# Score products on halves of the array's columns, every mask written ahead, and a new order of steps in an attention loop

## What is computed

```
h = x W^T + b + LoRA(x)
q, k, v = h @ ((qw - 8) * scales)      # per group of 128 rows; 32, 8, 8 heads of 128
q, k = rope(q), rope(k)                # by the token's place
scores = q k^T / sqrt(128), masked where key > query
ctx = softmax(scores) v
x = x + ctx @ ((qw_o - 8) * scales_o)
x = x + FFN(LoRA2(x))                  # layer norm, two layers with 8-bit rounding, GELU
```

## Time and profile before

| | |
|---|---|
| median of 3 runs | 568.68 us (568.56 to 568.96) |
| the profiled execution | 569.7 us, span 567.9 us |
| TensorE busy, clock granted | 542.2 us (95%), 1.00 |
| VectorE, ScalarE, GpSimd busy | 485.0, 363.0, 400.2 us |
| DMA | 51.93 MB, mean 91 GB/s |

### The profile page before, as it was taken

How to read it: one execution, slowest core, us unless ns; L and a number is a source line. 1 busy time by engine, 2 the same in 40 slices (tenths; PEclk the granted TensorE clock), 3 DMA queues, 4 the chain that set the end, 5 groups by cost and what they waited for, 6 DMA issues and landing times.

```text
span 567.9 us, 10485 instructions
## 1 busy us (share of the span) xinstructions
PE 542.2 (95%) x3135; PEld 425.0 (75%) x3139; DVE 485.0 (85%) x626; ACT 363.0 (64%) x940; POOL 400.2 (70%) x410
## 2 busy tenths in 40 slices
PE   6999989999999999999999999999999999987885
PEld 3555768888888888888888888888888888865432
DVE  3553859997999799979997999799979998976897
ACT  3573567657665766576657665766576656665895
POOL 3005577799779977997799779977997799851063
PEclk9999999999999999999999999999999999999999
DMA  8752435422442244124512451245124312200003
GB/s 289 180 123 76 123 88 160 113 56 58 137 124 51 62 133 126 43 65 133 128 37 66 134 132 33 61 136 136 34 61 135 97 34 61 80 1 1 1 20 129
DMA packets 38172, 51.93 MB, mean 91 GB/s; under 512 B 12100, under 2 KB 20452, under 8 KB 38148
## 3 DMA queue, kind: packets, MB, share of 16 engines
q1 hardware_dynamic: 35652, 46.94, 31.3%
q10 hardware_dynamic: 2016, 3.48, 1.9%
q0 software_dynamic: 480, 1.22, 0.7%
HBM read 28.55 MB, written 2.10 MB: 54 GB/s over the span
## 4 chain that ended last, share of the span: by engine, by line
PE 80%; DVE 10%; issue 3%; DMA 2%; ACT 2%; POOL 2%; ACTq 0%; SPq 0%; DVEq 0%; POOLq 0%
PE pair L1378 23%; PE pair L1379 23%; PE flow L1367 9%; PE flow L1494 9%; PE flow L1486 4%; PE pair L1315 4%; DVE y_max L1191 2%; DVE raw_v L1081 1%; PE flow L1372 1%; DMA stage<-in_x 1%; PE flow L1315 1%; DMA swap_q<-raw_q 1%; DVE rope_c L1203 1%; DVE ctx_lo L1102 1%; DVE probs L1203 1%
## 5 line engine op out<-in xcount | busy, mean ns | idle before, releaser
L1095 DVE SCALAR_TENSOR_TENSOR accT<-pair,so_now,accT 128x1024 f32<-128x1024 f32 x125 | 157.2, 1274 | 14.8 <-PE pair L1379 13.9
L1081 DVE SCALAR_TENSOR_TENSOR raw_q<-pair,sc_now,raw_q 128x1024 f32<-128x1024 f32 x90 | 115.4, 1283 | 6.2 <-ACT raw_q L777 2.8
L560 POOL TENSOR_TENSOR probs<-probs,rowinv 128x512 f32<-128x512 f32 x64 | 66.8, 1044 | 65.4 <-DVE rowinv L1068 65.4
L722 ACT ACTIVATE probs<-flow,negmax 128x128 f32<-128x128 f32 x248 | 87.6, 369 | 32.8 <-DVE negmax L1049 32.8
L1378 PE MATMUL pair<-ctx_hi,wo 128*128 128x512 f32 x256 | 104.9, 410 | 2.8 <-issue 1.5
L1378 PE MATMUL pair<-h_hi,wq 128*128 128x512 f32 x240 | 100.0, 417 | 0.3 <-ACT raw_q L777 0.3
L1379 PE MATMUL pair<-ctx_lo,wo 128*128 128x512 f32 x256 | 100.2, 392 | 0.0
L1379 PE MATMUL pair<-h_lo,wq 128*128 128x512 f32 x240 | 94.1, 392 | 0.0
L529 POOL TENSOR_TENSOR rope_s<-swap_q,consts 128x512 f32<-128x512 f32 x62 | 80.2, 1293 | 9.2 <-DMA swap_q<-raw_q 9.2
L541 POOL TENSOR_TENSOR qT<-rope_c,rope_s 128x512 f32<-128x512 f32 x62 | 79.3, 1280 | 4.4
L529 POOL TENSOR_TENSOR rope_c<-raw_q,consts 128x512 f32<-128x512 f32 x62 | 78.8, 1293 | 0.0
(11 more groups left out here) (242 smaller groups left out, 966.3 us busy)
## 6 DMA issues: line engine op xcount, KB each, us to landing
swap_q<-raw_q SPq DMA_DIRECT2D x62, 256.0 KB, 3.7
wq_i<-in_L_attn_qw_q SPq DMA_DIRECT2D x8, 1024.0 KB, 5.6
wo_i<-in_L_attn_qw_o SPq DMA_DIRECT2D x32, 256.0 KB, 2.6
swap_k<-raw_k SPq DMA_DIRECT2D x14, 256.0 KB, 3.6
wkv_i<-in_L_attn_qw_k SPq DMA_DIRECT2D x8, 256.0 KB, 3.7
wkv_i<-in_L_attn_qw_v SPq DMA_DIRECT2D x8, 256.0 KB, 4.0
stage<-in_x ACTq DMA_DIRECT2D x4, 256.0 KB, 5.7
probs<-in_L_ffn_w ACTq DMA_DIRECT2D x4, 256.0 KB, 8.2
```

What stands on the lines that cost most here:

```text
L560: pool.tensor_tensor(pr, pr, rowinv[:, f, :].unsqueeze(2).broadcast_to([P, HB, P]), ALU.mult).then_inc(probs_done, 1)
L722: e = act.activation(probs[:, 0, f, seq(b)], bank[:, seq(b)], ACT.Exp, bias=negmax[:, f, b:b + 1], accum_out=rowsum[:, f, b:b + 1])
L1081: dve.scalar_tensor_tensor(out=into, in0=flat(pair[pair_of(h, (kind, j), last)][:, :, :]), scalar=sc_now[:, scale_slot(kind, h), j:j + 1], ...
L1095: dve.scalar_tensor_tensor(out=a, in0=flat(pair[pair_of(h, (O, c), last)][:, :, :]), scalar=so_now[:, (h if c == 0 else h - 1) % 2, c:c + ...
```

## The change

- **Scores on column halves.** Per pair of sequences b, b+1 four products: the later 64 queries of each over all 128 keys, then the earlier 64 over the first 64 keys. The tokens of even sequences stand turned (64 to 127 first), so that the two later halves fall on different column halves of the array and of the bank. The masked quarter isn't computed.
- **Turned tokens.** x of the even sequences is loaded, and their output stored, in two halves; the tables of cosine, sine and mask get a second, turned copy (1035 instead of 651 columns).
- **Mask.** ScalarE seeds it for all heads in the loop (SEEDED = 4): in head 3 after the copy of the values. The mask product stays for the first and the last scores.
- **Order.** PERIOD, and the lists of all five engines, are written out anew, head by head.

```
+            else:
+                for here, there in zip(HALVES, halves_of(b)):
+                    eng.dma_start(x_nat[b][here, :], x[b, there, :]).then_inc(d_x[b], 16)
...
-        SEEDED = REP - 1
+        SEEDED = REP
...
-        PERIOD = [[(Q, 0), (O, 1), (Q, 1), (Q, 2), (Q, 3), (K, 0), (O, 2), (O, 3), (K, 1), (O, 0)],
-                  [(Q, 0), (O, 1), (Q, 1), (Q, 2), (Q, 3), (K, 2), (O, 2), (O, 3), (K, 3), (O, 0)],
-                  [(Q, 0), (O, 1), (Q, 1), (Q, 2), (Q, 3), (V, 0), (V, 1), (O, 2), (O, 3), (V, 2), (O, 0)],
-                  [(Q, 0), (O, 1), (Q, 1), (Q, 2), (Q, 3), (V, 3), (O, 2), (O, 3), (O, 0)]]
+        PERIOD = [[(Q, 0), (O, 1), (Q, 1), (Q, 2), (K, 0), (Q, 3), (O, 2), (K, 1), (O, 3), (O, 0)],
+                  [(Q, 0), (O, 1), (Q, 1), (Q, 2), (K, 2), (O, 2), (Q, 3), (O, 3), (K, 3), (O, 0)],
+                  [(Q, 0), (O, 1), (V, 0), (Q, 1), (Q, 2), (V, 1), (O, 2), (Q, 3), (O, 3), (V, 2), (O, 0)],
+                  [(Q, 0), (O, 1), (Q, 1), (V, 3), (Q, 2), (Q, 3), (O, 2), (O, 3), (O, 0)]]
...
+                def tile(b, late):
+
+                    rows, keys = halves_of(b)[late], slice(0, P) if late else halves_of(b)[0]
+                    t = HB * f + b
+                    return pe.matmul(bank[rows, seq(b)][:, keys], qT[:, par, seq(t)][:, rows], kT[:, seq(t)][:, keys],
+                                     start=False, stop=True, skip_group_check=True)
+
+                for b in range(0, HB, 2):
+                    tile(b, 1)
+                    tile(b + 1, 1)
+                    tile(b + 1, 0)
+                    mm = tile(b, 0)
...
+                        if h == 3:
+                            act.wait_ge(v_kept, 2 * (g + 1) + f + 1)
+                        else:
+                            act.wait_ge(ctx_split, 2 * n + f + 1)
+                        act.activation(per_pair(flow[f][:, :]), on_each_pair(tri), ACT.Copy).then_inc(mask_seeded, 1)
```

More of the change, by code:

```diff
@@ L816, in body @@
[L816 to L826 removed]
+                        round_kv()
@@ L1498, in values_ahead @@
                     def values_ahead(f):
-                        if h == 3 and not last:
-                            if f == 0:
-                                pe.wait_ge(dve_drained, drains_by(g, h, (V, 3), first, last))
-                            pe.wait_ge(ctx_split, 2 * n + f + 1)
-                            turn_values(f, flow[f])
+                        if last:
+                            return
+                        if f == 0:
+                            pe.wait_ge(dve_drained, drains_by(g, h, (V, 3), first, last))
+                        pe.wait_ge(ctx_split, 2 * n + f + 1)
+                        for b in range(HB):
+                            mm = pe.matmul(flow[f][:, seq(b)], raw_v[:, f, seq(b)], ident, is_transpose=True,
+                                           start=(b == 0), stop=(b == HB - 1), skip_group_check=True)
+                        mm.then_inc(vT_done, 1)
                     def scores_ahead(f):
@@ L1533, in body @@
                         context(0)
-                    else:
+                        context(1)
+                        scores_ahead(0)
+                        scores_ahead(1)
+                        output(0)
+                    elif last and h == 3:
+                        output(1)
+                        output(2)
+                        output(3)
+                        turn_probs(0)
+                        turn_probs(1)
+                        context(0)
+                        context(1)
+                        output(0)
+                    elif h == 0:
+                        project(Q, 0)
+                        output(1)
+                        project(Q, 1)
+                        project(Q, 2)
+                        project(K, 0)
+                        turn_probs(0)
+                        turn_probs(1)
+                        project(Q, 3)
+                        context(0)
+                        context(1)
+                        output(2)
+                        project(K, 1)
+                        output(3)
+                        scores_ahead(0)
+                        scores_ahead(1)
+                        output(0)
+                    elif h == 1:
+                        project(Q, 0)
+                        output(1)
+                        project(Q, 1)
+                        project(Q, 2)
+                        project(K, 2)
+                        turn_probs(0)
+                        output(2)
@@ L1542, in body @@
                         project(V, 0)
+                        project(Q, 1)
+                        project(Q, 2)
+                        turn_probs(0)
                         project(V, 1)
-                    if h == 3:
-                        project(V, 3)
-                    context(1)
-                    if not (last and h >= 2):
+                        output(2)
+                        project(Q, 3)
+                        turn_probs(1)
+                        context(0)
+                        context(1)
@@ L1562, in body @@
-                    output(0)
-                    if not (last and h == 2):
+                        scores_ahead(0)
+                        values_ahead(1)
+                        output(0)
                         scores_ahead(1)
```

497 lines of the change are left out of this document (349 added, 148 removed).

## The result

The change made the kernel slower: **575.31 us** (574.86 to 575.80, 4 runs) against 568.76 us (568.56 to 568.96, 4 runs), a ratio of 1.0115 [1.0098, 1.0133]. The forecast of 564.2 us had the wrong sign, and the time lies above its range. The profiled execution took 575.8 us with a span of 573.7, so the two traces differ by 5.8 us of span.

What follows compares the result with a forecast made beforehand. TensorE's own stream was taken as the bound, busy 95% of the span. From 568.7 us: loop -5.5, early scores +0.3, last head's pair +0.1, input loads +0.6, giving 564.2; range 558.5 to 572.

Steps and rivals of the forecast that it cites:

- The input loads: At the start: two issues of about 0.45 us instead of one for sequences 0 and 2; 0 to 1.5 late, taken 0.6.
- sign of being wrong: The prediction called itself wrong if the period moved over 1.5 us either way, or the start shifted by more than 1.5.
- The last group: First and last groups counted as 1.2 groups' worth beside six whole ones, each 0.77 us less: -5.5 us in all.
- The tiles: Score products on column halves: a half takes 0.68 us against 0.89, 1.7 us less in a group.
- the visits: Entering and leaving the column form: 0.148 us in, 0.20 out, 5 visits, 1.7 us a group, eating the tiles' gain.
- rival 4: Score halves, issue pace: 16 records at 57 ns make 0.91 us, tiles bring nothing, kernel 577; chance 0.05.
- The mask: In the loop: two products fewer, -0.45 us on TensorE a group; head 3's half 1 seed 0.4 us late.
- The value turn: Head 3's value turns: the 0.5 us wait for V's last drain goes, since that drain now lies earlier.
- The stalls: TensorE's waits in a group of the new order: 1.2 us, from turns, contexts, V's last step and the mask seed.
- rival 3: Loop: small waits take back TensorE's gain, period stays at 57.0 us, kernel 569.2; chance 0.15.
- 56.0 to 56.7: Sign expected in the profile after: a loop period of 56.0 to 56.7 us.
- Rival 2: Loop: VectorE falls 1 us further behind, TensorE waits for buffer pairs; period 57.4 us, kernel 572; chance 0.20.

Runs made afterwards that it cites:

- the best version: Changed kernel, x loaded whole and turned by TensorE's transposes, last group's buffer pairs given by steps present, head 3's mask product back; q step not moved: 568.59 us, ratio 0.9984.
- all_mended_product: Changed kernel, x loaded whole and turned by TensorE, last group's pairs by steps present and q step earlier, head 3's mask product back: 568.60 us against 569.52, ratio 0.9977.
- after_whole_scores: Changed kernel with each score product on the whole array again, order, tokens and tables kept: 574.87 us, ratio 1.0086 to the kernel before.
- before_tiles: Kernel before, in its own order and masks, with column halves, turned tokens and split loads: 580.43 us, ratio 1.0201.
- after_last_rotated: Changed kernel, in the last group q's last step ahead of the turns and buffer pairs given out by the steps present: 573.20 us, ratio 1.0058 to the kernel before.
- turned_identity: Changed kernel with x loaded whole and even sequences turned by TensorE's transposes with an exchanged identity: 570.11 us, ratio 1.0006 to the kernel before.

## Why the prediction was wrong

**The input loads: the step that failed most.** The forecast took 0.6 us, "0 to 1.5 late", for two more issues of 0.45 on ScalarE's queue. The runs showed 4.3. Two things were left out. One is that both transfers of a sequence have to land: the first turns of x started at 6.91 us where they had at 4.90, and those of sequence 1 at 9.87 where they had at 6.57. The other is that GpSimd waits for sequence 1 before it issues any of the other four loads. I read the chain up to the fourth x and stopped there; TensorE didn't wait for the fourth after the change. GpSimd's path ended, before, with an issue at about 8.6 and 7.2 us to landing, at 15.8, only 1.2 ahead of the turn that uses it; after, at 21.16. The step had a mechanism that covered one queue, where the change touched two. It also had TensorE turning at the old pace; in the trace its turns took twice as long, and by itself that path was 3.96 late. What makes the two transfers land so late isn't settled: sequence 1 was issued at 2.50 instead of 1.67 and landed 3.3 us later, so that the issues explain 0.8; the rest lies in the transfers. The prediction's own sign of being wrong, a start that shifts by more than 1.5, came.

**The last group: a step that wasn't there.** The forecast counted "1.2 worth in the first and last" as whole gains. The last group has no K and V steps, and the new order leans on them: they stand between exponentials and turns. It lost 2.7 us, of which the pairs make 0.8 (the wait of 0.86 us) and the mask 0.4; 1.5 are left in the best version, and their cause stays open. The waits for the normalisation (1.07 and 0.42) look like the missing K steps, but giving TensorE the q step there, with the pairs mended, removed these waits and not the loss: other waits took their place (all_mended_product, 37.43 against 37.22 without the moved step). So filling those gaps isn't enough; what bounds this group wasn't isolated.

**The tiles: right.** "A half done in 0.68, 0.148 in and 0.20 out" came as 0.67, 0.146 and 0.203. The forecast that the visits eat the tiles' gain is shown by after_whole_scores (net 0.09 us a group) and before_tiles. The Trainium skill (TensorEngine Tiling (Array Packing), Theoretical Speedup) promises up to 2x; the half went from 0.89 to 0.67, 1.3x, which is no more than the left-out quarter of the work gives, before the drains that its Key Properties name took it back. The trace agrees with the drain: a visit costs 0.35 us, in which the prediction counted the first weight loads too.

**The issue pace: rival 4 fell.** 16 records in 0.67 us are 42 ns each, below the 57 ns of the earlier trace rows. The Trainium skill (TensorE: Matmul & The Clock Gate, section "Wait — 56ns, not 53.3ns?") has about 62 ns per matmul with hardware decoding off; 42 ns is below that, so that figure doesn't bound this kernel.

**The mask: right in kind, wrong in size.** The forecast had "-0.45 on TensorE" against "0.4 us late", a gain of 0.05. The wait was 0.63 beyond the way in, and the product put back gave 0.22 us a group. The term that was mis-sized is the chain behind the value turn. The step that failed is "0.20 + 0.60 + 0.60 + 0.10": copy and seed took their 0.60 each, but from the seed's end (246.95 + 0.60 = 247.55) to the scores at 247.77 it was 0.22 and not 0.10, and the whole chain (0.20 + 0.63 + 0.60 + 0.22) 1.65 where I had 1.50.

**The value turn: right.** Its wait of 0.5 has gone.

**The stalls: too few.** With 36.4 of steps, 5.4 of score halves (8 x 0.67), 1.7 of visits (5 x 0.35), 7.1 of contexts, 3.55 of turns and 0.89 of value turns, a group's stream is 55.1, so 56.79 has 1.7 us of stalls where I had 1.2. Of the 0.5, 0.2 are the mask's, and 0.25 stand in front of one turn of half 0 that waits for GpSimd's normalisation (280.85, 0.48 behind a product that streams for 0.23), which the walk didn't have. The period came out 0.29 shorter instead of 0.77, which over 7.2 groups is 3.4 us of the miss; 56.79 lies between the forecast's 56.35 and the 57.0 of rival 3, outside the 56.0 to 56.7 that was to show the forecast.

**The tail: not foreseen.** The stretch in which the granted clock fell, in the windows view of after:

```profile
530.00:534.50 4.50, 4.49 (x26) 1.79 (x19) 3.38 (x11) 3.54 (x10) 0.00 (x0) 1.00 0.00 0
534.50:538.00 3.50, 3.28 (x13) 2.04 (x13) 3.10 (x10) 2.58 (x5) 0.00 (x0) 0.51 0.00 0
```

For 3.4 us the clock is at its lower level, 1.2 GHz (0.51 of 2.4), after a stretch in which TensorE was busy without a break. The same seven products and the turns behind them, first before, then after:

```profile
530.45 1.67 PE L1644 MATMUL pair<-ffT,ident_b 128*128 128x512 bf16 x7
...
533.81 0.66 PE L1605 MATMUL pair<-consts,accT 128*128 128x128 f32 x4 [0.50 <-DVE stage L1181]
```

```profile
536.26 2.54 PE L1934 MATMUL pair<-ffT,ident_b 128*128 128x512 bf16 x7 [0.22 <-issue]
...
539.78 0.66 PE L1895 MATMUL pair<-consts,accT 128*128 128x128 f32 x4
```

They take 0.87 us longer. The lag of TensorE's turns grew by 1.0 over this stretch (529.31 and 534.29 before it, 533.81 and 539.78 behind it), and 5.88 - 4.98 = 0.9 of it is there at the end. after_last_rotated has no dip in its tail, and turned_identity has one, at 537 us. Executions of the kernel before differ in this way too: of 20 on one chip the mean granted clock was 0.995 to 1.000, and the one at 0.995 took 571.42 us where one at 1.000 took 568.60. So 0.9 us of the profiled difference need not come from the change.

**The sum.** Against the forecast: start 4.3 less the 0.6 allowed, +3.7; loop +3.4; last group +2.7; tail +1.0 (0.9 of it the clock); together 10.8. Less the 0.4 that the forecast had added for scores outside the loop, which are inside these stretches, and with the 0.7 by which the medians lie further apart than the profiled spans, that is the 11.1 us missed. Rival 2, the one on the other side, named 572 through buffer pairs in the loop; in the group shown no step waited for a pair by more than 0.2 us. Pairs did bite, in the last group, which it hadn't named.

## What to carry to other kernels

Price a change of a load by who waits for its landing, on every queue, not by its issue time: here one wait of GpSimd for one of eight loads passed a late landing on to four more. Reorder rows where work is done on them anyway (here a transpose with an exchanged identity, free) rather than in the transfer. And when steps are absent from the first or last pass of a loop, walk that pass on its own: a buffer rotation laid out for the full pass collided there (0.8 us), and another 1.5 us were lost there for which no edit was found.

## What the runs showed of the hardware

- Column halves in fp32 run side by side: 16 records of 64 columns in 0.67 us, with weight loads of 0.137 each on different halves overlapping. Entering the form costs 0.146 us and leaving it 0.203.
- Two transfers of 64 rows landed later than one of 128: sequence 0 let TensorE start at 6.91 us instead of 4.90 (6.49 to 7.92 in the seven traces with split loads, 4.09 to 5.25 in the seven with whole ones). An issue of a half took 0.62 to 0.67 us on ScalarE's queue where the whole one took 0.45 to 0.50. The bytes were the same.
- TensorE's granted clock fell to half for 3.4 us in a busy tail and cost 0.9 us; it came in some executions and not in others of similar kernels. At a granted clock of 0.50 four fp32 turns took 0.86 us (before_tiles), at 1.00 they took 0.44 to 0.46 (before).
